# Transposed one-hots made on VectorE, convolution pipeline over eight PSUM banks, attention rows of 65 floats in two buffers

## The reference

```python
def _cgconv(x, edge_index, Wf, bf, Ws, bs):            # twice, relu after each
    j, i = (edge_index[0], edge_index[1])
    z = jnp.concatenate([x[i], x[j]], axis=-1)
    m = jax.nn.sigmoid(z @ Wf + bf) * jax.nn.softplus(z @ Ws + bs)
    return x + jax.ops.segment_sum(m, i, num_segments=x.shape[0])

def gat_conv(x, src, dst, edge_attr, W, We, att_s, att_d, att_e, bias):   # twice, self loops added
    xl = x @ W
    alpha = leaky_relu(a_src[src2] + a_dst[dst2] + a_edge, 0.2)
    ex = jnp.exp(alpha - segment_max(alpha, dst2)[dst2])
    p = ex / segment_sum(ex, dst2)[dst2]
    return segment_sum(xl[src2] * p[..., None], dst2) + bias
```

## Time and profile before

| | us |
|---|---|
| three runs: median (lowest, highest) | 11949.66 (11938.69, 12019.32) |
| the profiled execution, and its span from first to last instruction | 11948.91, 11947.2 |
| PE, PEld, DVE, ACT, POOL busy | 5556.7, 4608.2, 4117.8, 3660.0, 6476.5 |

### The profile page before, as it was taken

The page is one execution under the profiler, slowest core; times in us unless marked ns, Lnnn a source line. Parts: engine busy times, 40 slices in busy tenths (PEclk is TensorE's granted clock), DMA queues, the critical chain, the costliest instruction groups (busy, mean ns, idle before and its releaser), DMA issues. The chain is left out here.

```text
span 11947.2 us, 145647 instructions
## 1 busy us (share of the span) xinstructions
PE 5556.7 (47%) x28523; PEld 4608.2 (39%) x28524; DVE 4117.8 (34%) x12227; ACT 3660.0 (31%) x9441; POOL 6476.5 (54%) x6800
## 2 busy tenths in 40 slices
PE   2666566656656666666513333333342333333332
PEld 1444444544444545455413233333331333333332
DVE  6333333333334444444412222222251222322226
ACT  1444444444444444444302111121120111111112
POOL 0555555555466666666356555565516556556561
PEclk6788778887877777777655555555555555555555
DMA  4212112212222222222222222222212222222221
GB/s 115 59 56 57 53 54 57 59 53 56 57 72 65 65 64 64 65 64 65 64 65 61 56 61 59 58 62 56 61 29 62 60 57 60 57 59 61 56 61 34
DMA packets 565320, 716.87 MB, mean 60 GB/s; under 512 B 203990, under 2 KB 454602, under 8 KB 563595
## 3 DMA queue, kind: packets, MB, share of 16 engines
q0 software_dynamic: 214032, 440.06, 14.4%
q1 hardware_dynamic: 345932, 261.83, 7.5%
q10 hardware_dynamic: 5193, 13.44, 0.3%
HBM read 627.86 MB, written 86.89 MB: 60 GB/s over the span
## 5 line engine op out<-in xcount | busy, mean ns | idle before, releaser
L641 POOL DMA_INDIRECT big<-q_table,idx_stage x3328 | 3215.7, 966 | 2213.9 <-PE bank L759 959.5
L1032 POOL DMA_INDIRECT big<-xl_table,idx_stage x3328 | 3209.9, 965 | 2218.3 <-ACT msg L1174 1242.7
L1228 PE MATMUL bank<-msg,onehot 128*128 128x66 f32 x6656 | 1661.6, 412 | 2010.1 <-issue 1667.2
L1228 PEld LDWEIGHTS bank<-msg,onehot 128*128 128x128 f32 x6656 | 1528.2, 323 | 2043.5 <-issue 1786.7
L527 DVE TENSOR_TENSOR onehot<-iota,dst_rel 128x512 f32<-128x512 f32 x1664 | 1148.7, 694 | 2850.6 <-remote 1745.0
L1138 DVE TENSOR_TENSOR wide<-wide,bank 128x66 f32 x3328 | 742.3, 223 | 3432.1 <-issue 1670.8
L767 PE MATMUL bank<-msg,onehot 128*128 128x67 f32 (+1 forms) x6656 | 1075.5, 317 | 915.3 <-issue 776.6
L759 PEld LDWEIGHTS bank<-big,onehot_t 128*128 128x128 f32 x6656 | 1177.0, 249 | 612.2 <-issue 612.2
L767 PEld LDWEIGHTS bank<-msg,onehot 128*128 128x128 f32 x6656 | 1038.4, 238 | 963.1 <-issue 874.2
L756 PE MATMUL bank<-big,ident 128*128 128x512 f32 x1664 | 1245.2, 840 | 38.1 <-DMA big<-q_table,idx_stage 30.4
L1172 ACT ACTIVATE msg<-work 128x8 f32 (+1 forms) x832 | 172.7, 208 | 3217.1 <-remote 2897.3
(11 more groups left out here) (212 smaller groups left out, 3800.2 us busy)
## 6 DMA issues: line engine op xcount, KB each, us to landing
big<-turned SPq DMA_DIRECT2D x832, 128.0 KB
big<-q_table,idx_stage POOLq DMA_INDIRECT x3328
turned<-wide SPq DMA_DIRECT2D x416, 128.0 KB
wide<-turned SPq DMA_DIRECT2D x416, 128.0 KB
big<-xl_table,idx_stage POOLq DMA_INDIRECT x3328
big<-in_edge_attr ACTq DMA_DIRECT2D x12, 1024.0 KB, 4.8
q_table<-wide SPq DMA_DIRECT2D x12, 1024.0 KB, 5.1
xl_table<-big SPq DMA_DIRECT2D x12, 520.0 KB, 4.5
```

What stands on the lines that cost most here:

```text
L641: pool.indirect_dma_start(out=ring[:, u, s % GROUP, :], out_offset=None, in_=k.q_table, in_offset=bass.IndirectOffsetOnAxis(ap=k.idx_stage ...
L1032: pool.indirect_dma_start(out=buf[:, s, :], out_offset=None, in_=k.xl_table, in_offset=bass.IndirectOffsetOnAxis(ap=k.idx_stage[:, s:s + 1 ...
L1228: last_one = nc.tensor.matmul(sum_bank[c % UNROLL][:, i * P:i * P + C + 2], k.onehot[:, c % UNROLL, i, :], k.msg[:, c % UNROLL, i, 0:C + 2 ...
```

## The change

VectorE now makes the transposed one-hot itself. The setup stores `rel` as bf16 rows in DRAM (`rel_rows`, one row of 128 a step, with 13 more VectorE operations and 13 more DMAs). In every edge stage SP fetches the rows of two groups at once, broadcast to all 128 partitions (256 KB), and VectorE compares them with the partition's number in one `tensor_scalar` of 128x512 a group: to f32 in the convolutions (four slots), to bf16 in the attention layers (four slots). TensorE's transposes, ScalarE's two copies, the tensor `turned` with its stores and loads, and the zero fill of `xl_table`'s spare columns go.

The convolutions' loop body is 8 groups instead of 4. `form` writes to four PSUM banks (0 to 3) and `segment_sum` to four others (4 to 7); the scratch `soft` has four slots instead of two. The stages' lags change, `onehot` is built behind `message`, and waits of distance two become waits of distance four. The ring of gathered rows keeps its four slots. In the attention layers a row of `xl_table` has 65 floats instead of 128, there are two buffers of 128 slots, and the gather of batch b waits for the messages of batch b - 2 instead of b - 1. VectorE's group there has one operation more.

```diff
-TW = 2 * C
+TW = C + 1
...
-        self.turned = nc.dram_tensor("turned", (GROUPS, P, GROUP * P), BF16, kind="Internal").ap()
+        self.rel_rows = nc.dram_tensor("rel_rows", (STEPS, P), BF16, kind="Internal").ap()
...
             for b in range(NBATCH):
                 v.wait_ge(s_g[b % 2], 16 * (b // 2 + 1))
...
+                wait(v, s_kept[b % 2], 16 * (b // 2))
+                nc.vector.tensor_scalar(rel_bf[b % 2], gath[b % 2][:, KEY:KEY + P], off[:, b:b + 1], None, ALU.subtract).then_inc(s_rb, 1)
...
+def rel_row(k, pair):
+
+    return k.rel_rows.rearrange("(q s) e -> q (s e)", s=2 * GROUP)[ds(pair, 1), :].broadcast_to([P, 2 * GROUP * P])
...
+    rel = rel_slots(k.wide[:, 0:CG_PAIRS * GROUP * P], CG_PAIRS)
+    at = CG_PAIRS * GROUP * P
+    turned = k.wide[:, at:at + UNROLL * GROUP * P].rearrange("p (u i c) -> p u i c", u=UNROLL, c=P)
+
+    soft = k.work[:, 0:UNROLL * GROUP * P].rearrange("p (u i c) -> p u i c", u=UNROLL, c=2 * C)
+    pre = [k.psum[j][:, :].rearrange("p (i c) -> p i c", c=2 * C) for j in range(4)]
+    agg = k.psum[4:8]
...
-            def keep(it):
-                for u in range(UNROLL):
-                    sp.wait_ge(s_Tb, it * UNROLL + u + 1)
+
+            def fetch(it):
+                for q in range(CG_PAIRS):
+                    wait(sp, s_T, (it - 1) * CG_UNROLL + 2 * q + 2 if not isinstance(it, int) or it else 0)
                     sp.sem_inc(s_turn, 1)
...
+                    sp.dma_start(rel[q], rel_row(k, it * CG_PAIRS + q)).then_inc(s_rel[q], 16)
...
-                n = counts(v, it * UNROLL, -4, 3)
-
-                def onehot(c):
-                    wait(v, s_agg, n[c - 3])
-                    build_onehot(nc, k, k.onehot[:, c % UNROLL], it * ITER + c * GROUP).then_inc(s_S, 1)
+                n = counts(v, it * CG_UNROLL, -10, 5)
+
+                def onehot_t(c):
+                    if c % 2 == 0:
+                        v.wait_ge(s_rel[c // 2], it * 16 + 16)
+                    wait(v, s_X, n[c - 3])
+                    nc.vector.tensor_scalar(turned[:, c % UNROLL, :, :].rearrange("p i c -> p (i c)"),
+                                            rel[c // 2][:, c % 2 * GROUP * P:(c % 2 + 1) * GROUP * P],
+                                            k.iota_col[:, :], None, ALU.is_equal).then_inc(s_T, 1)
 
...
                 def message(c):
-                    j = c % 2
+                    j = c % UNROLL
                     wait(v, s_sig, n[c + 1])
                     wait(v, s_softs, n[c + 1])
-
-                    nc.vector.tensor_tensor(k.msg[:, c % UNROLL, :, 0:C], soft[:, j, :, f_half], soft[:, j, :, s_half], ALU.mult).then_inc(s_msg, 1)
+                    wait(v, s_agg, n[c - 3])
+                    nc.vector.tensor_tensor(k.msg[:, j, :, 0:C], soft[:, j, :, f_half], soft[:, j, :, s_half], ALU.mult).then_inc(s_msg, 1)
+                    build_onehot(nc, k, k.onehot[:, j], it * (CG_UNROLL * GROUP) + c * GROUP).then_inc(s_S, 1)
 
                 def accumulate(c):
...
-                for u in range(UNROLL):
-                    stages(u, first, last, (0, onehot), (2, softs), (3, message), (4, accumulate))
-            pipelined(v, ITERS, iteration)
+                for u in range(CG_UNROLL):
+                    stages(u, first, last, (0, onehot_t), (3, softs), (4, message), (7, accumulate))
+            pipelined(v, CG_ITERS, iteration)
...
-                def copy_t(c):
-                    if layer == 0:
-                        wait(act, s_T, n[c + 1])
-                        from_ = k.psum[c % 2][:, :].rearrange("p (i c) -> p i c", c=P)
-                    else:
-                        act.wait_ge(s_hold[c], it * 16 + 16)
-                        from_ = slots[c]
-                    wait(act, s_X, n[c - 1])
-                    nc.scalar.activation(k.onehot_t[:, c % 2, :, :], from_, ACT.Copy).then_inc(s_Tc, 1)
-
-                def copy_bf(c):
-                    if layer == 0:
-                        wait(act, s_hold[c], it * 16)
-                        nc.scalar.activation(slots[c], k.psum[c % 2][:, :].rearrange("p (i c) -> p i c", c=P),
-                                             ACT.Copy).then_inc(s_Tb, 1)
+                n = counts(act, it * CG_UNROLL, -6, 6)
 
                 def logs(c):
...
-                for u in range(UNROLL):
-                    stages(u, first, last, (0, copy_t), (2, sigmoids), (1, logs), (0, copy_bf))
-            pipelined(act, ITERS, iteration)
+                        wait(act, s_agg, n[c - 3])
+                        nc.scalar.activation(k.msg[:, j, :, C:C + 2], k.ae[:, ds(it * (CG_UNROLL * GROUP) + c * GROUP, GROUP), :], ACT.Copy)
+                    nc.scalar.activation(soft[:, j, :, f_half], soft[:, j, :, f_half], ACT.Exp).then_inc(s_sig, 1)
+
...
-                def transposes(c):
-                    if layer == 1:
-                        return
-                    wait(pe, s_S, n[c + 1])
-                    wait(pe, s_Tb, n[c - 1])
+                n = counts(pe, it * CG_UNROLL, -8, 7)
...
+                def form(c):
+
+                    j = c % UNROLL
+                    at = load_offsets(k, pe, TAB_ROW, it * (CG_UNROLL * GROUP) + c * GROUP, GROUP, 2 * C)
+                    pe.wait_ge(s_row[j], gathered + (16 * GROUP * (c // UNROLL + 1) + row_base[j]))
+                    wait(pe, s_softs, n[c - 3])
+                    nc.tensor.matmul(k.psum[j][:, :], k.ident[:, :], ring[:, j].rearrange("p i c -> p (i c)"), start=True, stop=False)
+                    wait(pe, s_T, n[c + 1])
                     for i in range(GROUP):
-                        last_one = nc.tensor.transpose(k.psum[c % 2][:, i * P:(i + 1) * P], k.onehot[:, c % UNROLL, i, :], k.ident[:, :])
-                    last_one.then_inc(s_T, 1)
-
-                def form(c):
-
-                    j, slot = c % 2, c % UNROLL
-                    at = load_offsets(k, pe, TAB_ROW, it * ITER + c * GROUP, GROUP, 2 * C)
-                    pe.wait_ge(s_row[slot], gathered + (16 * GROUP * (1 if c >= 0 else 0) + row_base[slot]))
-                    wait(pe, s_softs, n[c - 1])
-                    nc.tensor.matmul(k.psum[2 + j][:, :], k.ident[:, :], ring[:, slot].rearrange("p i c -> p (i c)"), start=True, stop=False)
-                    wait(pe, s_Tc, n[c + 1])
-                    for i in range(GROUP):
-                        last_one = nc.tensor.matmul(k.psum[2 + j][:, i * P:(i + 1) * P], k.onehot_t[:, j, i, :],
+                        last_one = nc.tensor.matmul(k.psum[j][:, i * P:(i + 1) * P], turned[:, j, i, :],
                                                     p_tab[:, ds(at[i], 2 * C)], start=False, stop=i == GROUP - 1)
                     last_one.then_inc(s_X, 1)
 
                 def segment_sum(c):
+                    j = c % UNROLL
                     wait(pe, s_msg, n[c + 1])
-                    wait(pe, s_acc, n[c])
+                    wait(pe, s_S, n[c + 1])
+                    wait(pe, s_acc, n[c - 2])
                     for i in range(GROUP):
-                        last_one = nc.tensor.matmul(k.psum[4 + c % 2][:, i * P:i * P + width], k.onehot[:, c % UNROLL, i, :],
-                                                    k.msg[:, c % UNROLL, i, 0:width], start=True, stop=True)
+                        last_one = nc.tensor.matmul(agg[j][:, i * P:i * P + width], k.onehot[:, j, i, :],
+                                                    k.msg[:, j, i, 0:width], start=True, stop=True)
                     last_one.then_inc(s_agg, 1)
 
-                for u in range(UNROLL):
-                    stages(u, first, last, (0, transposes), (1, form), (3, segment_sum))
+                for u in range(CG_UNROLL):
+                    stages(u, first, last, (1, form), (5, segment_sum))
...
-    buf = k.big[:, 0:P * TW].rearrange("p (s c) -> p s c", c=TW)
+    buf = [k.big[:, i * P * TW:(i + 1) * P * TW].rearrange("p (s c) -> p s c", c=TW) for i in range(2)]
...
             def fetch(it):
-                for u in range(UNROLL):
-                    wait(sp, a_X, (it - 1) * UNROLL + u + 1 if not isinstance(it, int) or it else 0)
+                for q in range(PAIRS):
+                    wait(sp, a_T, (it - 1) * UNROLL + 2 * q + 2 if not isinstance(it, int) or it else 0)
                     sp.sem_inc(s_turn, 1)
-                    sp.dma_start(flat(slots[u]), turned_rows(k, it, u)).then_inc(s_held[u], 16)
+                    sp.dma_start(rel_pair[q], rel_row(k, it * PAIRS + q)).then_inc(s_rel[q], 16)
...
-                        wait(pool, e_m, (b - 1) * BGROUPS + (s // GROUP + 1))
+                        wait(pool, e_m, (b - 2) * BGROUPS + (s // GROUP + 1))
...
+            def turn_onehot(c, it, n):
+                if c % 2 == 0:
+                    v.wait_ge(s_rel[c // 2], it * 16 + 16)
+                wait(v, a_X, n[c - 3])
+                nc.vector.tensor_scalar(turned[:, c, :, :].rearrange("p i c -> p (i c)"),
```

(17 more changed lines are left out.)

96 lines of the change are left out of this document (44 added, 52 removed).

## The result

| | before | changed |
|---|---|---|
| median (lowest, highest), us | 11978.51 (11938.69, 12019.32), 4 runs | 11561.15 (11552.12, 11568.8), 4 runs |
| ratio, 95% interval | | 0.9651 [0.961, 0.9692] |
| profiled execution, its span, us | 11948.91, 11947.2 | 11567.74, 11566.0 |

What follows compares the result with a forecast made beforehand. POOL's gathers were the floor, with waits for engines that catch up only in its pauses; 11,949 - 565 - 154 (convolutions) + 64 (attention) + 5 (setup) + 20 (port) = 11,319, say 11,320 us; range 10,400 to 12,000.

Steps and rivals of the forecast that it cites:

- What bounds the kernel: All stages: POOL's gathers are a floor of 2113 us each; above it POOL waits for engines slowed beside gathers.
- the alternation: Convolution 1: POOL makes eight gathers in a row, then pauses while the other engines catch up; 12.1 us per two groups.
- the terms for the port and the setup: Shared memory port, all four stages: +20 us from lengthened gathers and delays; setup's extra operations and store: +5 us.
- Convolutions: Both convolutions: three groups a POOL run, 2.0 us pause, 5.75 us a group; -565 us in convolution 0, -154 in 1.
- 2402 us: Each convolution: 416 groups at 5.75 us, 2392, plus 10 for a longer pipeline end.
- the collisions rival: Edge stages: each one-input comparison may hold the port, 0.64 us x 1664 = 1065 us, total 12,380; chance 0.12.
- The fill agrees with it: Port rule: a gather under way when VectorE's 5.53 us fill began lasted 7.30 us instead of 0.95, taken as support.
- The comparison: VectorE's new 128x512 operation: 0.44 us a group, costing nothing while VectorE's group stays under POOL's run.
- Attention: Attention stages: 2113 + 11 x 52 us, then two batches without gathers at 102 each; 2889, +32 us a stage.
- Rows of 260 bytes: Attention gathers: 260 bytes a partition instead of 512 change nothing; landing 1 us longer would add 22 us over both stages.
- boundaries hidden: Attention: softmax runs beside gathers that have credit, saving 286 us a stage, total 10,750; chance 0.13.
- POOL bounds everywhere: All stages: POOL's gathers alone set the time, total 9,600 us; chance 0.07.

Runs made afterwards that it cites:

- the second traces: Kernel before and changed kernel, both unaltered, run again for their traces on a later chip: 9842.22 us and 9477.68 us (the latter 0.9627 of 9838.56).

## Why the prediction was right, and where not

**What bounds the kernel: right for its chip, and only for it.** On the chip of the trace POOL stops for the others, and the alternation continued after the change. On the other chips POOL stops for nobody in the convolutions. The trace alone could not have told that; its waits were real, but they were a property of where or when it ran. Their cause, why the others' steps come 1.4 us apart beside gathers there and not on the other chips, stays open: no experiment met it. That continuous gathers by themselves do it is refuted as a general rule: 1664 gathers without a pause on the other chips leave no such steps in the convolutions. On the first chip gathers had a part in it all the same: the slow steps lie in the long runs of POOL, and the batch without gathers is as quick as elsewhere. So the account of the gain, longer runs and fewer pauses, rests on reading two traces; no experiment varied banks, lags or buffers on that chip, and what each of them gave there isn't shown.

**The sum** was 248 us too low: 99 and 89 us in the convolutions, 45 and 39 in attention, less 24 of the terms for the port and the setup, which stood beside the stages (what the port cost is in the stages' times).

**Convolutions: the course as forecast, size 0.7.** Forecast -565 and -154, measured -466 and -65. Runs of POOL were to have 12 gathers; of the runs in convolution 0, 48 have 12 and 54 have 16. Pauses: 128 with 2.4 us, 302 us, where the sum had 139 of 2.0 us, 277; in convolution 1 120, 287 us. Two terms were mis-sized, and they are the steps that failed. First what VectorE holds of the gathers: "+20 us" for all four stages. The time from one gather to the next within a run rose from 1.274 to 1.310 us and from 1.270 to 1.316: 60 + 76 = 136 us in the convolutions. Part of that is a row misread: the prediction took the 0.942 and 0.947 of the earlier trace rows for middle and mean, and so put what VectorE holds at 8 us a stage, where the mean of 0.966 over the shortest of 0.942 says 40. The other part is that I scaled a kernel whose VectorE worked mostly in POOL's pauses; longer runs put more of its work beside the gathers, the two-input one-hot above all (93 and 100 us held now). Second, 2402 us was the time of the gathers, and I took it from the stages' 2967 and 2556, which hold 26 and 18 us before and after them. The pauses themselves were 25 and 10 us over their 277. The prediction named gathers of more than 1.0 us on average as a sign of being wrong, and that came true by a hair in the convolutions: 0.999 and 1.004, together 1.002 us.

**The rule weighed there.** The Trainium skill, "SBUF — State Buffer", section "Who interferes with whom", says that a VectorE operation with two inputs from SBUF contends with a GpSimd instruction that reads SBUF. The experiment with four one-input operations agrees (75 us held down to 33). The same section of the Trainium skill infers that `tensor_tensor` doesn't stall the writing of descriptors. The 1.21 us of the gathers beside the one-hot speak against that, though the trace doesn't show which part of a gather waited, its reading of row numbers or its writing of descriptors. I had weighed the Trainium skill's rule on one-input operations in a two-port mode, the collisions rival; the comparison does hold gathers, but by 15 to 24 us a convolution, not by 0.64 us a group. "The fill agrees with it" said too much: no run shows that the fill works in such a mode, so the 7.30 us of the earlier trace rows are one held gather and no test of that rule.

**The comparison** took 0.513 us to f32 and 0.383 to bf16, where 0.44 stood for both. The 0.07 us a group more stayed under POOL's run and are no term of the sum.

**Attention: the course as forecast, the loss more than double.** Forecast +32 a stage, measured +77 and +71. The first boundary came behind 256 gathers, as said. Eleven boundaries instead of twelve, of 26.6 us each; 310 us of pauses within the sums, 28 a batch where 26 stood; gathers 2720 against 2685 us; and 106 us more behind the last gather, where 102 were forecast for the second batch without POOL. The 35 us of the gathers are most of what was missed. On the other chips the rival "boundaries hidden" is what happened (its price was 286 us a stage by boundaries of 26 us; they are 17.1 there, and it was 203), together with "POOL bounds everywhere" (9,600 forecast, 9,478 measured). Both had 0.2 together. The forecast stayed in its range because the result was measured where the trace had been; on the other chips the changed kernel's 9,478 us lie far outside it.

**Rows of 260 bytes:** the mean gather in attention stays at 0.960 us (0.965 before), no effect to be seen in the result. The profile gives no time of landing for these gathers.

## What to carry to other kernels

Before a wait is explained by the kernel, run the same kernel on a second chip: here the same change gives 3.5% in its first runs through its convolutions, and 3.7% on the chip that ran it again through its buffer, while the other half of the change costs a little in either case. When one engine's instructions are the floor, as POOL's gathers are, count what its neighbours do to the length of each: VectorE work that took 0.51 us a group longer but had one input from SBUF instead of two was worth 1% of the whole. A second buffer pays only when the side that fills it is the late one.

## What the runs showed of the hardware

- One kernel took 11,950 us in its first runs and 9838 to 9850 us on four chips later, with an equal setup, equal VectorE work (4118 and 4120 us busy) and an equally long attention batch where no gathers run beside it (95 and 93 us). The medians of the four agree within 0.13%.
- A VectorE operation of 128x512 with two inputs from SBUF lengthens the record of a gather beside it from 0.947 to 1.21 us in the mean, and to 1.26 where the gather begins in the operation's first 0.45 us; one that starts over 0.3 us behind the gather's start leaves it at 0.946. One with one input (128x128) gives 0.963.
- After a fill of its own that it waits for, POOL began the next fill 0.14 us later and a gather 0.93 us later.
- In convolution 0, on the chip of the second traces, TensorE's granted clock stood at 0.92 of full speed in the mean with the transposes and at 0.81 without them, at nearly equal busy time (1605 and 1543 us). It cost nothing, since POOL bounds that stage.
